# An audio tower on one core: two VectorE blocks merged, signs multiplied before they are searched for zeros, and the order inside a slot rewritten

## The chip, the cores and the metric

The kernel runs on one core of one Trainium2 chip. The metric is the device time of one execution in microseconds (us). PE is TensorE, DVE is VectorE, ACT is ScalarE.

## What is computed

Sixteen audio clips of 250 frames become a residual stream `h` (16 x 250 x 192). It passes top-k attention (A), a mixture of eight experts (B), a linear attention (C) and a mixture of sixteen experts (D). The change touches A and B.

```python
# A, per batch: 12 heads of 16, 250 queries by 250 keys
attn = jnp.einsum('bhnd,bhmd->bhnm', q, k) * SCALE
kth = jax.lax.top_k(attn, 100)[0][..., -1:]
attn = jax.nn.softmax(jnp.where(attn >= kth, attn, -jnp.inf), axis=-1)
h = h + einsum('bhnm,bhmd->bhnd', attn, v) @ w_proj + b_proj
# B: routed, on layernorm(h), the best 2 of 8 experts
gu = jnp.minimum(x @ Wgu + bgu, 7.0)
act = (jnp.maximum(up, -7.0) + 1.0) * gate * sigmoid(1.702 * gate)
h = h + sum over the chosen experts of score * (act @ Wd + bd)
```

## The kernel before

After the front end (to about 97 us) A and B run together in one program that every engine walks in the same order: `slots()`. A **unit** is four heads of one batch, so there are 48 units, and a **period** of four slots (s = 0 to 3) brings each unit one stage further. With k the age of a unit in periods:

- k = 0: PE computes scores, ACT copies them to `s_sb`.
- k = 1, slot 1: VectorE's `a_start` takes each row's maximum (`L1174`, 8 x 250 scores per partition) and from it and the mean a first threshold `first`; its last instruction (`L1187`) raises `start_set`, on which ACT waits.
- k = 1 to 4: ACT's `a_count` (`L919`) forms sign(threshold - score) for all scores and sums it; VectorE's `a_steps` (slot 0) moves the thresholds by interpolation. The fourth time the signs are kept, in bf16, in `mk` (8 x 250 per partition).
- k = 4, slot 1: VectorE's `a_rank`. `L1245` reads all 2000 signs, marks those equal to zero (a score that is exactly the threshold) and sums the marks in `ties`; `rank` says how far the count is from 100; seven small instructions turn both into `bad`, which is 0 where the threshold can be used. PE sums `bad` over the partitions (`L547`), VectorE copies the sum to `badi` (`a_flag`, slot 3).
- k = 5: `a_full` (slot 0) loads `badi` in a register and branches around an exact search that is needed if it isn't 0; then `a_hot` (`L1309`), and in every slot `a_top`: the 16 largest below the threshold by MAX, MATCH_REPLACE and MAX (`L1324`, `L1327`, `L1330`) for two of the eight rows. In even slots it begins with `L1320`, which prepares four rows. In odd slots it ends with `L1334` and `L1335`, which pick the 100th value (`kth`). `a_keep` (`L1344`) masks the exponentials with it; PE transposes the result (`L557`), ACT copies it, PE multiplies by v (`L571`).

In the same slots runs B, one of twelve steps per slot: PE multiplies up (`L457` with `w_b_g`, `w_b_u`), VectorE clips (`m0_first`: `L1425`, `L1428`), ACT takes the tanh, VectorE combines (`m0_act` `L1446`, `m0_weigh` `L1437`, `m0_hidden` `L1455`), PE multiplies down (`m0_down`, `L634`). `m0_act` and `m0_hidden` work on the step before that of `m0_first`. Twice per batch `residual` adds a result to `h` in five steps: add into `hb` (`L1139`), copy to `h` (`L1141`), two bn_stats, two bn_aggr, copy to `mv` (`L1117`).

The order on VectorE within a slot is that of the code. `Chain` guards instructions that use each other's results: `mark` lets an instruction raise a semaphore, `wait(but=k)` waits for all marked ones except the last k, `link` is both, `start` clears the semaphore (the row `ISA` in the listings below). `carry` is a one-element memset on which a wait rides.

Of the kernel before, what the change touches and what calls it, by code (L numbers as in the profile page):

```python
# [15 lines left out]
ALU = mybir.AluOpType  # L16
# [39 lines left out]
SHIFT = (WINDOW - 0.5) / 2  # L56
SLOPE = 1.0 / (2.7 * 193.2)
# [9 lines left out]
class Chain:  # L67
# [11 lines left out]
    def mark(self, ins):  # L79
        self.k += 1  # L80
        ins.then_inc(self.sem, 1)

# [79 lines left out]
def build(nc, d, out):  # L162
    with ExitStack() as ctx:
# [51 lines left out]
        st6 = sb("st6", [P, 2, 6])  # L215
        mvb = sb("mvb", [P, 2, 2])
# [35 lines left out]
        bad = own([P, 1], late)  # L252
        junk = own([P, UT * N // 2], late).bitcast(mybir.dt.bfloat16).rearrange("p (t n) -> p t n", t=UT)
# [839 lines left out]
        def _(dv):  # L1093
# [50 lines left out]

            dv.wait_ge(w_tok_ps, 1)
# [22 lines left out]
            def a_start(u):  # L1168

                n, ub = u[3:]  # L1170
                dv.wait_ge(s_set, UH * (n + 1))
                carry()
                top.start()
                top.link(dv.tensor_reduce(rowmax[:, ub, :], s_sb[:, ub, :, 0:N], AX.X, ALU.max))  # L1174
                way, mx = tiny[:, 0, :], rowmax[:, ub, :]
                top.mark(dv.tensor_scalar(nmx[:, ub, :], mx, -scale, None, ALU.mult))
                q = 1 - n_par(u)
                first, end = thr[:, q, 0, :], ends[:, q, :, 0, :]
                top.mark(dv.memset(end[:, Y_LO, :], FAR))
                top.mark(dv.memset(end[:, Y_HI, :], -FAR))  # L1180

                top.link(dv.scalar_tensor_tensor(way, s_sb[:, ub, :, N], -1.0 / N, mx, ALU.mult, ALU.add))
                top.link(dv.scalar_tensor_tensor(first, way, GUESS - 1.0, mx, ALU.mult, ALU.add))
                top.mark(dv.scalar_tensor_tensor(end[:, T_LO, :], way, -FAR * SLOPE, first,
                                                 ALU.mult, ALU.add))
                top.wait()
                dv.scalar_tensor_tensor(end[:, T_HI, :], way, FAR * SLOPE, first,  # L1187
                                        ALU.mult, ALU.add).then_inc(start_set, 1)

            def a_steps(b, g, p):  # L1190
# [15 lines left out]
                carry()  # L1206
                top.start()
# [25 lines left out]
            def a_rank(u):  # L1233


                n, ub = u[3:]
                m = n_par(u)
                dv.wait_ge(signs_set[3], n + 1)

                started = n + 4  # L1240
# [451 lines left out]
```

## Time and profile before

| | |
|---|---|
| runs of the kernel | 2815.48, 2818.47, 2827.93 us (median 2818.47) |
| the profiled execution | 2823.92 us, its span 2821.8 us |
| mean granted TensorE clock of the span | 0.825 |
| busy over the span | PE 2506.4 us (89%), DVE 1948.4 us (69%), ACT 1531.7 us (54%) |

The span has three parts: the front end, A with B (to about 1850 us), then C and D. The share of an engine over the whole says little; it has to be read by part. An instruction on VectorE can start before the one ahead of it has ended, so what one costs in a row of independent instructions is the distance between starts, not its duration.

### The profile page before, as it was taken

The page shows a single profiled execution, that of the slowest core. Times are in us where ns is not written, and L with a number is a line of the kernel's source. Part 1 is how long each engine was busy: PE and PEld are TensorE (multiplying, and loading weights), DVE is VectorE, ACT ScalarE, POOL GpSimd, SP SyncE. Part 2 cuts the span into 40 slices and gives each one's busy share as a digit, 9 for nine tenths or more (in the row PEclk, how much of TensorE's full clock was granted, in tenths as well). Part 3 has the DMA queues.
Part 4 walks back from the last instruction along what each step waited for, and adds up shares of the span by engine and source line. Part 5 has one row for each costly group of instructions (what it writes and reads, how often), then busy time and mean ns, then how long its engine had stood idle before and what let it go on. Part 6 is the DMA issues. An engine that isn't in the chain of part 4 may idle for free.

```text
span 2821.8 us, 39986 instructions
## 1 busy us (share of the span) xinstructions
PE 2506.4 (89%) x11650; PEld 2110.6 (75%) x11650; DVE 1948.4 (69%) x6490; ACT 1531.7 (54%) x4856; POOL 72.5 (3%) x45
## 2 busy tenths in 40 slices
PE   7778799898898898988888877899999899999999
PEld 3456677677776777777777767778887799999998
DVE  3278899999999999999999999864444232222222
ACT  1498887777777777777776774211111222222222
POOL 0000000000000000000000000000000110011110
PEclk9755567867778778778768777899999899999999
DMA  3000000000000000000000010130000000000000
GB/s 118 0 1 1 1 19 16 12 19 16 12 20 16 12 19 16 12 19 16 12 19 16 12 19 17 27 107 1 0 0 0 1 7 6 6 3 6 6 6 9
DMA packets 35000, 44.10 MB, mean 16 GB/s; under 512 B 6054, under 2 KB 33676, under 8 KB 34060
## 3 DMA queue, kind: packets, MB, share of 16 engines
q1 hardware_dynamic: 32208, 38.57, 5.4%
q10 hardware_dynamic: 2592, 3.33, 0.4%
q8 instruction: 69, 1.13, 0.2%
q14 instruction: 131, 1.07, 0.1%
HBM read 38.43 MB, written 3.20 MB: 15 GB/s over the span
## 4 chain that ended last, share of the span: by engine, by line
PE 41%; DVE 41%; issue 9%; ACT 6%; POOL 1%; DVEq 1%; DMA 0%; SPq 0%; ACTq 0%; POOLq 0%
PE bank L457 18%; PE bank L706 7%; DVE late L1327 4%; DVE late L1324 4%; DVE late L1344 3%; ACT late L919 3%; DVE late L1330 3%; DVE late L1245 3%; DVE late L1174 3%; DVE late L1320 3%; PE bank L536 2%; DVE extra L1455 2%; DVE extra L1446 2%; PE bank L767 2%; PE bank L571 2%
## 5 line engine op out<-in xcount | busy, mean ns | idle before, releaser
L919 ACT ACTIVATE late<-arena,late 125x250 bf16<-125x250 f32 x1152 | 561.3, 492 | 0.0
L1517 DVE TENSOR_TENSOR pair<-pair,arena 128x500 f32<-128x500 f32 x192 | 139.3, 726 | 443.1 <-PE bank L706 349.3
L571 PEld LDWEIGHTS bank<-vaug,late 125*125 125x125 f32 x1536 | 252.5, 240 | 167.1 <-ACT late L929 113.0
L457 PE MATMUL bank<-xT,late 128*128 128x250 f32 x1536 | 360.9, 378 | 0.0
L571 PE MATMUL bank<-vaug,late 125*125 125x17 f32 x1536 | 240.8, 293 | 120.8 <-ACT late L929 78.6
L536 PE MATMUL bank<-late 16*125 16x251 f32 x768 | 303.0, 530 | 21.3 <-ACT arena L896 20.4
L1033 ACT ACTIVATE pair<-bank 128x500 f32<-128x500 f32 x192 | 112.7, 587 | 382.5 <-PE bank L457 382.3
L457 PEld LDWEIGHTS bank<-xT,late 128*128 128x128 f32 x1536 | 287.0, 192 | 26.3
L706 PE MATMUL bank<-late,pair 128*125 128x192 f32 x1536 | 280.5, 326 | 0.0
L457 PE MATMUL bank<-extra,w_b_g 128*128 128x250 f32 x768 | 276.1, 495 | 0.8
L706 PEld LDWEIGHTS bank<-late,pair 128*125 128x125 f32 x1536 | 258.3, 187 | 9.5 <-DVE pair L1517 0.4
L457 PE MATMUL bank<-extra,w_b_u 128*128 128x250 f32 x768 | 255.2, 467 | 0.0
L937 ACT ACTIVATE late<-arena,late 125x250 f32<-125x250 f32 x384 | 171.2, 495 | 143.4 <-DVE late L1344 143.3
L557 PE MATMUL bank<-w_ident,late 125*125 125x125 f32 x768 | 164.6, 352 | 82.8 <-DVE late L1344 82.8
L536 PEld LDWEIGHTS bank<-late 16*125 16x125 f32 x768 | 172.4, 248 | 78.8 <-issue 31.4
L457 PEld LDWEIGHTS bank<-extra,w_b_g 128*128 128x128 f32 x768 | 176.4, 248 | 63.8 <-issue 33.9
L557 PEld LDWEIGHTS bank<-w_ident,late 125*125 125x125 f32 x768 | 147.9, 255 | 98.4 <-DVE late L1344 98.1
L919 ACT ACTIVATION_READ_ACCUMULATOR late<-arena,late 125x1 f32 x1152 | 220.1, 191 | 0.0
L457 PEld LDWEIGHTS bank<-extra,w_b_u 128*128 128x128 f32 x768 | 191.1, 249 | 34.9
L634 PE MATMUL bank<-w_b_d,extra 128*125 128x192 f32 x768 | 206.9, 402 | 0.6 <-DVE extra L1455 0.6
L919 ACT ACTIVATE pair<-arena,late 125x250 bf16<-125x250 f32 x384 | 187.7, 493 | 6.0 <-DVE late L1231 6.0
L1344 DVE SCALAR_TENSOR_TENSOR late<-arena,late 125x250 f32<-125x250 f32 x384 | 165.8, 474 | 3.8 <-DVE late L1335 0.5
(178 smaller groups left out, 3954.4 us busy)
## 6 DMA issues: line engine op xcount, KB each, us to landing
late<-comb_rows SPq DMA_DIRECT2D x128, 125.0 KB, 3.0
late<-comb_rows SPq DMA_DIRECT2D x128, 62.5 KB, 2.6
late<-in_d SPq DMA_DIRECT2D x1, 3072.0 KB, 9.9
out_h<-extra ACTq DMA_DIRECT2D x16, 187.5 KB
late<-in_d SPq DMA_DIRECT2D x1, 2304.0 KB, 14.9
arena<-in_frames SPq DMA_DIRECT2D x1, 1562.5 KB
w_b_g<-in_b_g SPq DMA_DIRECT2D x1, 1536.0 KB
w_b_u<-in_b_u SPq DMA_DIRECT2D x1, 1536.0 KB
```

What stands on the lines that cost most here:

```text
L457: ins = pe.matmul(dst, lhs(t), rhs(t), start=t == 0, stop=t == 1)
L536: ins = pe.matmul(bank[2][0:P, half * (N + 1):(half + 1) * (N + 1)], qk[r:r + DH, qk_slot(u), 0, half * P:half * P + P], qk[r:r + DH, qk_s ...
L557: ins = pe.transpose(bank[3][0:P, kh * N + half * P:kh * N + half * P + P], p_sb[:, s % 2, half, kh * P:kh * P + P], ident[0:P, 0:P])
L571: ins = pe.matmul(bank[4][0:P, at:at + VW], pT[:, s % 2, kh, half * P:half * P + P], vaug[:, p, kh, UH * g + s, :], start=kh == 0, stop=kh ...
L634: ins = pe.matmul(D[0:P, half * C:(half + 1) * C], hid0[:, s % 2, half * P:half * P + P], w["b_d"][:, s, :], start=False, stop=s == 11, sk ...
L706: ins = pe.matmul(D[0:P, half * C:(half + 1) * C], hid[:, s % 2, i, half * P:half * P + P], w["d_2"][:, 2 * s + i, :], start=(s == 0 and i ...
L919: ins = sc.activation(mk[:, n_par(u), t, :] if k == 3 else junk[:, t, :], s_sb[:, ub, t, 0:N], ACT.Sign, bias=thr[:, (n_par(u) + k + 1) % ...
L937: ins = sc.activation(e_sb[:, s % 2, half, :], s_sb[:, ub, t, 0:N], ACT.Exp, bias=nmx[:, ub, t:t + 1], scale=float(DH) ** -0.5)
L1324: top.mark(dv.max(m16[:, t, 0:8], work[:, t, :]))
L1327: top.mark(dv.match_replace(work[:, t, :], m16[:, t, 0:8], work[:, t, :], -BIG))
L1344: ins = dv.scalar_tensor_tensor(p_sb[:, s % 2, half, :], s_sb[:, ub, t, 0:N], kth[:, t:t + 1], e_sb[:, s % 2, half, :], ALU.is_ge, ALU.mult)
L1517: dv.tensor_tensor(hid[:, s % 2, :, :], gl[:, s % 2, :, :], c, ALU.mult).then_inc(hid_set[1], 1)
```

## The change

`a_start` and `a_rank` become one function, `a_start_and_rank`, whose instructions alternate; the search for zeros goes over products of four signs; the product is formed in two steps, 1000 and 500 wide. `a_load_flag` loads the register at the start of slot 0, ahead of `a_keep(last, 3)` and `a_steps`. `a_top` no longer waits at its end; `a_picked` and `a_thresholds` are its last two instructions, and `m0_act` comes between them. `m0_act`, `m0_weigh` and `m0_hidden` move from ahead of `a_top` to behind it. `add_to_h` takes the place of `residual` in A and B: it adds in place and writes `mv` without a copy. C keeps `residual`. Arithmetic on the other engines and their programs are the same.

```diff
+EDGE = (WINDOW / 2) ** 2 - ((WINDOW - 1) / 2) ** 2
...
+    def settle(self):
+        if self.k:
+            self.wait()
...
+            def add_to_h(ph, b, acc, ready, value, hs):
+                dv.wait_ge(ready, value)
+                hv = h[:, 2 * b:2 * b + 2, :].rearrange("p g c -> p (g c)")
+                dv.tensor_tensor(hv, hv, acc[0:P, 0:2 * C], ALU.add).then_inc(hs, 1)
+                stats.start()
+                dv.wait_ge(hs, b + 1)
+                ge(dv, stat_set[ph], b)
+                for half in (0, 1):
+                    stats.mark(dv.bn_stats(sums[ph - 1][:, half, :], h[:, 2 * b + half, :]))
+                stats.wait()
+                for half in (0, 1):
+                    ins = dv.bn_aggr(mv[ph][:, 2 * b + half, :], sums[ph - 1][:, half, :])
+                ins.then_inc(stat_set[ph], 1)
...
-            def a_start(u):
...
-            def a_rank(u):
...
+            def a_start_and_rank(u, r):
...
+                top.settle()
                 top.start()
+                if u:
...
+                    dv.wait_ge(s_set, UH * (n + 1))
+                    top.mark(dv.tensor_reduce(mx, s_sb[:, ub, :, 0:N], AX.X, ALU.max))
+                if r:
...
+                    dv.wait_ge(signs_set[3], nr + 1)
...
+                    four, two = UT * N // 2, UT * N // 4
+                    top.mark(dv.tensor_tensor(tied[:, 0:four], mks[:, 0:four], mks[:, four:2 * four], ALU.mult))
+                    top.mark(dv.tensor_scalar(rank[:, m, :], signs[:, 3, :], 0.5, TOPK - 1.0 - N / 2,
+                                              ALU.mult, ALU.add))
+                    top.wait(but=1)
+                    top.mark(dv.tensor_tensor(tied[:, four:four + two], tied[:, 0:two], tied[:, two:four], ALU.mult))
...
+                    top.wait(but=3 if u else 0)
+                    top.mark(dv.tensor_scalar(tied[:, four + two:2 * four], tied[:, four:four + two], 0.0, None,
+                                              ALU.is_equal, ALU.add, accum_out=ties[:]))
+                    top.mark(dv.scalar_tensor_tensor(places, rank[:, m, :], WINDOW - 1.0, rank[:, m, :],
+                                                     ALU.subtract, ALU.mult))
+                    top.wait(but=1)
+                    top.mark(dv.tensor_scalar(limit, ties[:], -SHIFT, EDGE, ALU.mult, ALU.add))
...
+                    top.mark(dv.tensor_scalar(spots[:], places, limit, None, ALU.is_ge, ALU.add, accum_out=outside))
...
+                    dv.scalar_tensor_tensor(bad[:], outside, FULL, ties[:],
+                                            ALU.mult, ALU.add).then_inc(bad_set, 1)
+                if u:
+                    top.wait()
+                    dv.scalar_tensor_tensor(end[:, T_HI, :], way, FAR * SLOPE, first,
+                                            ALU.mult, ALU.add).then_inc(start_set, 1)
...
+            def a_load_flag(u):
+                dv.wait_ge(bad_read, u[3] + 1)
+                dv.reg_load(flag, badi[0:1, 0:1])
...
                 if s == 0:
+                    if old:
+                        a_load_flag(old)
                     if last:
                         a_keep(last, 3)
...
                 if new:
                     m0_first(*new)
+                if old:
+                    a_top(old, s)
+                    if s % 2:
+                        a_picked(old, s)
                 if was:
                     m0_act(*was)
+                if old and s % 2:
+                    a_thresholds(old, s)
                 if new:
                     m0_weigh(*new)
                 if was:
                     m0_hidden(*was)
...
+                if old and s % 2:
+                    a_keep(old, s - 1)
+                if s == 1:
+                    a_start_and_rank(unit(i, g, p, 1), unit(i, g, p, 4))
```

VectorE, slot 1 of a period, from the masking (`L1344`) on; `late` holds the thresholds and small tiles, `pair` the signs, `arena` the scores. Before:

```order
L1344 SCALAR_TENSOR_TENSOR late<-arena,late 125x250
L1107 MEMSET carrier 1x1 [waits s_set]
L76 ISA
L1174 TENSOR_REDUCE late<-arena 125x8
L1176 TENSOR_SCALAR late<-late 125x8 [waits top_step]
...
L1187 SCALAR_TENSOR_TENSOR late<-late 125x8 [waits top_step]
L1107 MEMSET carrier 1x1 [waits start_set,signs_set3]
L76 ISA
L1245 TENSOR_SCALAR late<-pair 125x2000
L1247 TENSOR_SCALAR late<-late 125x8
L1251 TENSOR_SCALAR late<-late 125x8 [waits top_step]
```

After, at the same place:

```order
L1385 SCALAR_TENSOR_TENSOR late<-arena,late 125x250
L77 ISA [waits top_step]
L1247 TENSOR_REDUCE late<-arena 125x8 [waits s_set]
L1256 TENSOR_TENSOR late<-pair 125x1000 [waits signs_set3]
L1257 TENSOR_SCALAR late<-late 125x8
L1260 TENSOR_TENSOR late<-late 125x500 [waits top_step]
L1262 MEMSET late 125x8
L1263 MEMSET late 125x8
L1265 SCALAR_TENSOR_TENSOR late<-arena,late 125x8 [waits top_step]
L1268 TENSOR_SCALAR late<-late 125x500 [waits top_step]
L1270 SCALAR_TENSOR_TENSOR late<-late 125x8
L1273 TENSOR_SCALAR late<-late 125x1 [waits top_step]
```

The row of 2000 became rows of 1000, 500 and 500, with small instructions of both blocks between them. The rest of the block is six more small instructions; `bad` is the last but one of them, and the one that raises `start_set` is the last.

VectorE, an odd slot, from `m0_first` to the masking. Before:

```order
L1425 TENSOR_SCALAR late<-bank,w_b_bg 128x250 [waits gc_set,tanh_set,up_ps0,top_step]
L1428 TENSOR_SCALAR late<-bank,bup 128x250 [waits hid_set0]
L1446 SCALAR_TENSOR_TENSOR extra<-late 128x250 [waits hid_set0,gc_set,tanh_set]
L1437 TENSOR_TENSOR late<-late 128x250 [waits act_set,ring_set1,gate_set]
L1455 SCALAR_TENSOR_TENSOR extra<-late,extra 128x250 [waits down_ps0,u_set,act_set]
L76 ISA
L1324 MAX late<-late 125x8 x2
L1327 MATCH_REPLACE late<-late 125x250 [waits top_step] x2
L1330 MAX late<-late 125x8 [waits top_step] x2
L1334 TENSOR_TENSOR late<-hot,late 125x64 [waits top_step]
L1335 TENSOR_REDUCE late<-late 125x4 [waits top_step]
L1344 SCALAR_TENSOR_TENSOR late<-arena,late 125x250 [waits pt_ps,e_set,top_step]
```

After:

```order
L1466 TENSOR_SCALAR late<-bank,w_b_bg 128x250 [waits tanh_set,gc_set,up_ps0]
L1469 TENSOR_SCALAR late<-bank,bup 128x250 [waits hid_set0]
L77 ISA [waits top_step]
L1359 MAX late<-late 125x8 x2
L1362 MATCH_REPLACE late<-late 125x250 [waits top_step] x2
L1365 MAX late<-late 125x8 [waits top_step] x2
L1370 TENSOR_TENSOR late<-hot,late 125x64 [waits top_step]
L1487 SCALAR_TENSOR_TENSOR extra<-late 128x250 [waits hid_set0,gc_set,tanh_set]
L1375 TENSOR_REDUCE late<-late 125x4 [waits top_step]
L1478 TENSOR_TENSOR late<-late 128x250 [waits act_set,ring_set1,gate_set]
L1496 SCALAR_TENSOR_TENSOR extra<-late,extra 128x250 [waits down_ps0,u_set,act_set]
L1385 SCALAR_TENSOR_TENSOR late<-arena,late 125x250 [waits pt_ps,e_set,top_step]
```

The three instructions of B that follow `m0_first` (`L1446`, `L1437`, `L1455`; now `L1487`, `L1478`, `L1496`) moved behind the maxima, one of them into the gap of the chain that ends in the masking.

## Rows read from the trace of the kernel before

**Rows 1.** Busy time by stage; PEclk is the granted TensorE clock

```profile
core 0: us, PE busy (x) PEld busy (x) DVE busy (x) ACT busy (x) POOL busy (x), PEclk, DMA share, GB/s
170.00:280.00 110.00, 91.09 (x304) 70.69 (x304) 99.29 (x347) 95.64 (x343) 0.00 (x0) 0.53 0.00 1
800.00:1120.00 320.00, 280.40 (x1235) 230.49 (x1234) 301.06 (x1050) 242.86 (x831) 0.00 (x0) 0.78 0.07 16
1770.00:2820.00 1050.00, 997.51 (x5528) 904.54 (x5528) 397.17 (x1058) 254.30 (x510) 70.24 (x32) 0.97 0.04 12
```

**Rows 2.** Waits between 480 and 1656 us: us in total, times, longest

```profile
PE bank L557 <- DVE late L1344: 53.2, 29, 4.4
...
PE bank L571 <- DVE o_sb L1358: 38.7, 11, 4.8
```

**Rows 3.** The same view as rows 1 around one wait of TensorE

```profile
1016.00:1028.00 12.00, 12.00 (x69) 10.49 (x70) 11.36 (x33) 9.60 (x33) 0.00 (x0) 1.00 0.01 2
1035.00:1045.00 10.00, 7.22 (x20) 5.63 (x21) 8.88 (x38) 5.50 (x20) 0.00 (x0) 0.50 0.06 14
```

**Rows 4.** VectorE in order of time: start us, us; start and rank of one period

```profile
1015.69 2.23 DVE L1174 TENSOR_REDUCE late<-arena 125x8 f32<-125x2000 f32 x1
...
1019.07 2.24 DVE L1245 TENSOR_SCALAR_CACHE_REDUCE late<-pair 125x2000 bf16<-125x2000 bf16 x1
...
1021.23 0.17 DVE L1247 TENSOR_SCALAR late<-late 125x8 f32<-125x8 f32 x1
1021.44 0.17 DVE L1251 TENSOR_SCALAR late<-late 125x8 f32<-125x8 f32 x1
...
1022.51 0.87 DVE L1344 SCALAR_TENSOR_TENSOR late<-arena,late 125x250 f32<-125x250 f32 x2
```

**Rows 5.** The same view: small instructions without and with a wait between them

```profile
1039.26 0.17 DVE L1215 TENSOR_SCALAR side<-late 125x24 int32<-125x24 f32 x1
...
1039.34 0.17 DVE L1216 TENSOR_SCALAR side<-late 125x24 int32<-125x24 f32 x1
```

**Rows 6.** The same view: one residual with its statistics

```profile
1023.30 0.55 DVE L1139 TENSOR_TENSOR hb<-h,bank 125x384 f32<-125x384 f32 x1
1023.88 0.36 DVE L1141 COPY h<-hb 125x384 f32<-125x384 f32 x1
...
1025.20 0.48 DVE L1425 TENSOR_SCALAR late<-bank,w_b_bg 128x250 f32<-128x250 f32 x1
```

**Rows 7.** The same view: ends of an odd and of an even slot

```profile
1035.57 0.73 DVE L1330 MAX8 late<-late 125x8 f32<-125x250 f32 x2
1036.34 0.23 DVE L1334 TENSOR_TENSOR late<-hot,late 125x64 f32<-125x64 f32 x1
...
1036.85 0.87 DVE L1344 SCALAR_TENSOR_TENSOR late<-arena,late 125x250 f32<-125x250 f32 x2
...
1046.71 0.73 DVE L1330 MAX8 late<-late 125x8 f32<-125x250 f32 x2
1047.48 0.48 DVE L1425 TENSOR_SCALAR late<-bank,w_b_bg 128x250 f32<-128x250 f32 x1
```

**Rows 8.** The same view: before the branch of a_full

```profile
1040.94 0.18 DVE L1231 TENSOR_TENSOR late<-late 125x24 f32<-125x24 f32 x1
...
1041.96 0.29 DVE L1309 TENSOR_TENSOR hot<-w_iota,late 125x128 f32<-125x128 f32 x1 [0.84 <-issue]
```

**Rows 9.** VectorE groups until 1800 us, by form: busy us, mean ns, idle before

```profile
L1320 DVE SCALAR_TENSOR_TENSOR late<-pair,arena 125x1000 f32<-125x1000 bf16 x96 | 114.6, 1194 | 1.2 <-DVE hot L1309 0.2
L1245 DVE TENSOR_SCALAR_CACHE_REDUCE late<-pair 125x2000 bf16<-125x2000 bf16 x48 | 107.4, 2237 | 3.4 <-issue 0.4
```

**Rows 10.** VectorE, then TensorE, in order of time: one step of B and one wait

```profile
1026.63 0.41 DVE L1455 SCALAR_TENSOR_TENSOR extra<-late,extra 128x250 f32<-128x250 f32 x1
...
1032.62 0.89 PE L634 MATMUL bank<-w_b_d,extra 128*125 128x192 f32 x4
1037.78 1.20 PE L557 MATMUL bank<-w_ident,late 125*125 125x125 f32 x4 [4.26 <-DVE late L1344]
```

More of the change, by code:

```diff
@@ L215, in build @@
         st6 = sb("st6", [P, 2, 6])
+        sums = [sb(f"sums{i}", [P, 2, 6]) for i in range(2)]
         mvb = sb("mvb", [P, 2, 2])
@@ L252, in build @@
         bad = own([P, 1], late)
+        spots = sb("spots", [P, UT])
         junk = own([P, UT * N // 2], late).bitcast(mybir.dt.bfloat16).rearrange("p (t n) -> p t n", t=UT)
@@ L1166, in _ @@
             scale = float(DH) ** -0.5
-            def a_start(u):
[L1170 to L1188, printed above, removed]
             def a_steps(b, g, p):
@@ L1274, in a_full @@
                 m = n_par(u)
-                dv.wait_ge(bad_read, n + 1)
-                carry()
-                dv.reg_load(flag, badi[0:1, 0:1])
                 with dv.If_ne(flag, 0):
@@ L1307, in a_hot @@
                 m = n_par(u)
+                top.settle()
                 top.start()
@@ L1317, in a_top @@
                 m = n_par(u)
+                top.settle()
                 top.start()
@@ L1330, in a_top, with a_picked, a_thresholds @@
                     top.mark(dv.max(m16[:, t, 8:16], work[:, t, :]))
+            def a_picked(u, s):
                 top.wait()
-                if s % 2:
-                    two = slice(2 * s - 2, 2 * s + 2)
-                    top.link(dv.tensor_tensor(picked, hot[:, two, :], m16, ALU.mult))
-                    top.link(dv.tensor_reduce(kth[:, two], picked, AX.X, ALU.add))
+                top.mark(dv.tensor_tensor(picked, hot[:, 2 * s - 2:2 * s + 2, :], m16, ALU.mult))
+            def a_thresholds(u, s):
+                top.wait()
+                top.mark(dv.tensor_reduce(kth[:, 2 * s - 2:2 * s + 2], picked, AX.X, ALU.add))
             def a_keep(u, s):
                 n, ub = u[3:]
+                top.wait()
                 dv.wait_ge(e_set, UH * n + s + 1)
@@ L1471, in _ @@
                 if b is not None:
-                    residual(2, b, bank[6], down_ps[0], 12 * b + 12, h_set["B"])
+                    add_to_h(2, b, bank[6], down_ps[0], 12 * b + 12, h_set["B"])
                 b = at_slot(T, LG_AT + 1)
@@ L1486, in _ @@
                     m0_hidden(*was)
-                if old:
-                    a_top(old, s)
-                    if s % 2:
-                        a_keep(old, s - 1)
-                if s == 1 and unit(i, g, p, 1):
-                    a_start(unit(i, g, p, 1))
-                if s == 1 and unit(i, g, p, 4):
-                    a_rank(unit(i, g, p, 4))
+                if old and s % 2:
+                    a_keep(old, s - 1)
+                if s == 1:
+                    a_start_and_rank(unit(i, g, p, 1), unit(i, g, p, 4))
                 if s == 3 and unit(i, g, p, 4):
@@ L1497, in _ @@
                 if g == 0 and s == 2 and has(i - 3):
-                    residual(1, i - 3, bank[0], proj_ps[0], i - 2, h_set["A"])
+                    add_to_h(1, i - 3, bank[0], proj_ps[0], i - 2, h_set["A"])
                 b = at_slot(T, X_AT - 1)
```

47 lines of the change are left out of this document (27 added, 20 removed).

## The prediction, made before the changed kernel ran

> **What bounds the kernel now.** First the busy time by stage [rows 1]. From 170 us to about 1770 us VectorE is busy 90 to 94% of the time, TensorE 83 to 88%, ScalarE 76 to 87%. What VectorE is short of 100% there is made of gaps of 0.03 to 0.1 us behind waits on its own instructions; no wait for another engine in the rows of its timeline. So VectorE sets the pace of A and B. After 1770 us TensorE is busy 95% at a granted clock of 0.97 and VectorE 38%: nothing that VectorE saves there comes back, and before 170 us VectorE waits for ScalarE's signs. The stage in which a saving counts is 1600 us long.
>
> Second, what TensorE has in reserve, because it is next. Between 480 and 1656 us it waits 53.2 us for the masking and 38.7 us for `divide`, the latter 11 times, once per batch [rows 2]. A batch is three units, so that is 92 us in about 33 units, **2.8 us per unit**. Third, the clock. TensorE runs at full speed while it is busy (1.00 from 1016 to 1028 us), and after a wait of 4.26 us [rows 10] the next ten microseconds are granted 0.50, the lower of its two levels, 1.2 GHz [rows 3]. Its waits are therefore dearer than they look, and fewer waits would make it faster.
>
> **The change part by part**, in time of VectorE, per unit or slot. The unit of account is the distance between starts. A small instruction behind a wait on the one before it starts 0.20 us after it (1021.23 to 1021.44 in [rows 4]); without one 0.08 us (1039.26 to 1039.34 in [rows 5]).
>
> *Start and rank.* Before: from `L1174` at 1015.69 to the masking at 1022.51, 6.82 us [rows 4]. The search over 2000 signs takes 2.24 us of it, the maximum 2.23; the rest is a chain of linked small instructions. After: the maximum, 2.15 (next start); then the product of 1000 signs. The trace has no bf16 x bf16 product. Upper bound: `L1320`, 1000 elements in 1.19 us [rows 9]; with 2.24 for 2000 this is 1.04 per 1000 and 0.15 fixed. Lower bound: twice that rate, 0.67 us, as the copy of 384 (0.36) against the sum of 384 out of a bank (0.55) shows that VectorE can stream at double rate [rows 6]. I take the lower, since both inputs and the output are 2 bytes wide and the doubling is seen here even for 4-byte data. Product: 0.67 and 0.03 for the wait; the second, 500 wide, 0.26 + 0.15 = 0.41; then two memsets and `way` in its shadow, 0.13 beyond its next start; the search over 500 at single rate (it carries a sum, and `L1245` with its sum ran at single rate), 0.67, with the read of the sum 0.08; then `limit`, `first`, `nmx`, `spots` with its sum, `T_LO`, `bad`, `T_HI`, of which each has a neighbour to cover its wait: about 0.8. Sum 2.15 + 0.70 + 0.33 + 0.21 + 0.70 + 0.8 = 4.9 us, 1.9 less than 6.82. With the single rate for both products it is 0.78 more, 1.1 saved. Of 48 periods with a start, 44 have also a rank and lie behind 170 us: **84 us**. Three ranks without a start save about 1.1 each, since the chain of seven behind the search becomes four: **3 us**.
>
> The Trainium skill's page "VectorE: DVE Perf Modes", in its section on the perf-mode tier table, gives tensor_tensor on bf16 in SBUF double rate (1224 ns against 2293 ns for 2048 elements). No row here shows it for a product; by it the 4.9 stands, by the nearest row, `L1320`, it would be 5.7.
>
> *Sums into h.* Before, start to start, 1.90 us [rows 6]. After: 0.55 + 0.03, two statistics and their wait 0.65, two aggregates 0.18 = 1.4. Saved 0.48: the copy to `h` (0.36) and that to `mv`. About 28 of 32 lie in the stage: **13 us**. `h_set` also comes 0.4 us earlier for TensorE.
>
> *Odd slots.* Before, from the last pair of maxima at 1035.57 to the masking at 1036.85 are 1.28 us, of which the maxima hold 0.77 [rows 7]; the two linked instructions cost 0.51. After, the first starts 0.03 after the maxima end and the next instruction can follow after 0.15; the second, with `m0_act` between, 0.14. Saved 0.22, in the 82 odd slots in which B runs too: **18 us**. *Even slots.* The wait at the end of `a_top` (0.77 from 1046.71 to 1047.48) goes, since `m0_act` needs nothing of it: the start can be at 0.65. Saved 0.12 x 82: **10 us**.
>
> *The register.* Between `L1231` and `L1309` lie 1.0 us, 0.84 of it idle [rows 8], with the load of `badi` and a branch over the exact search. The branch stays. The load now stands right behind `a_flag`, whose result it waits for, and behind it on VectorE's queue stand the masking `a_keep(last, 3)` and all of `a_steps`; TensorE waits for that masking. So the load is moved from one bare spot to another, except in the third of the units in which `b_normalise` stands between. I take a third of the idle time, 0.3 us, in 16 units: **5 us**; bounds 0 and 0.35 x 48 = 17. The removed memsets (`carry`) overlap others and are counted at nothing.
>
> Sum: 84 + 3 + 13 + 18 + 10 + 5 = **133 us**, if all of VectorE's saving becomes time.
>
> *What takes some back.* Per unit of the steady stretch this is 1.9 + 0.3 + 0.44 + 0.24 + 0.1 = 3.0 us, a little over TensorE's 2.8. At an unchanged clock TensorE would bind, and 0.2 us x 33 units (7 us) be lost; and its waits are not evenly spread: only 29 masked heads of 132 in the stretch had one [rows 2]. In the others VectorE will sometimes find TensorE late. Against that stands the clock, which should fall less often. I take off 10%, 15 us in all. **Gain 118 us.** Of 2823.92 us (the profiled execution, span 2821.8) this leaves 2706; the median of the runs is 5.5 us lower, so the forecast for the median is **2700 us**, 4.2% faster.
>
> **The rivals.**
>
> *TensorE takes over.* For it: 88% busy, 2.8 us of reserve. If only half of the waits can be turned into time, because the clock stays at 0.78, the gain per unit is 1.4 to 1.8 us over 42 units, 60 to 75 us: 2750 us. Against it: all its waits end in VectorE's work, which comes earlier, and the clock recovers once it is busy [rows 3].
>
> *The products run at single rate.* 0.78 x 44 = 34 us less: 2734 us.
>
> *Order is worth nothing.* Then only removed work counts: per period 2.24 us of search become 0.67 + 0.41 + 0.67, three small instructions fewer (0.5), together about 1.0 x 44, and the copies, 13: 57 us, 2761 us. Against it stand 0.20 and 0.08 us in [rows 4, 5]. "VectorE: DVE Perf Modes" says this under "The DRAIN you can't avoid": chained operations pay the same with and without semaphores, so one should save operations, not waits. By that section the time would be this rival's; the rows disagree for instructions as small as these.
>
> *Slower: B's result comes late.* `m0_hidden` now stands behind `a_top`, in even slots 4.3 us later (1.2 for `L1320`, 3.1 for the rest). `m0_down` waits for it: in the shown slot it began 5.6 us after the result (1026.63 + 0.41 to 1032.62, [rows 10]), so 1.3 us would be left. If TensorE comes to both even slots too early, it waits there and its clock falls to 0.50; ten low microseconds as in [rows 3] cost it 5 us of work, so twice per unit 10 us, against 2.8 of reserve and 3.0 saved: such a unit gets 4.2 us longer. In every second unit of 42 that is 21 x 4.2 = 88 us more, less 59 us, the half of the gain: 2848 us. It decides from the point where the wait is longer than the one it has for the masking right after; against it, in odd slots the masking itself stands behind `m0_hidden`, so nothing is later than it was.
>
> That the change doesn't find what the old search found is no case: `rank * (rank - 15) >= 7.75 - 7.75 * ties` is the old test with 56.25 taken off both sides, and a product of four signs is zero if one is.
>
> **How the numbers follow.** Forecast 0.66; TensorE takes over 0.16; single rate 0.08; order worth nothing 0.05; slower 0.05. Own range of the forecast: full 133 us with the register's 12 more, 2673, to 2730. Reaching the second, third and fourth case the range is 2670 to 2762; the slower case and the outer tails are left out. A measurement can tell about 0.5% (14 us). Faster by more than that: 0.92; within 0.04; slower 0.04.
>
> **What would show it.** In the changed profile: the product of 1000 at 0.67 us (or 1.19); 4.9 us from the maximum's start to the masking; 1.4 us per sum into `h`; 0.15 us from the pick to `m0_act`; VectorE still over 90% busy to about 1650 us, TensorE above 92%, its clock there at 0.78 or higher. Wrong, if VectorE shows waits for `L457` of B's gate and up products or for the sum in bank 6, if TensorE waits at `L634` for `m0_hidden`, if the clock in the stretch is lower, or if ScalarE's counting waits for `start_set`, which is now raised last in its block, 1.8 us later against the maximum.

## The result, and the profile after

The changed kernel takes **2683.86 us** (median; 2682.34 to 2691.15) against 2823.2 us for the kernel before in the same comparison (2815.48 to 2829.24). The ratio is 0.9513, interval 0.948 to 0.9546: 4.9% faster, 139 us. The forecast was 2700 us, a gain of 118 us, with a range of 2670 to 2762. The profiled execution of the changed kernel took 2691.15 us, the slowest of its four, with a span of 2689.1 us.

The page of the changed kernel, its first rows and the granted clock in 40 slices:

```profile
span 2689.1 us, 39761 instructions
...
PE 2431.5 (90%) x11650; PEld 2052.7 (76%) x11650; DVE 1836.2 (68%) x6330; ACT 1527.3 (57%) x4856; POOL 72.7 (3%) x45
...
PEclk9975578888788878868877778999997999999999
```

Busy time by stage, the view of [rows 1]; A with B now ends 134 us earlier (last product of B at 1747 us instead of 1881), so the last stretch is taken from 1650:

```profile
core 0: us, PE busy (x) PEld busy (x) DVE busy (x) ACT busy (x) POOL busy (x), PEclk, DMA share, GB/s
170.00:280.00 110.00, 90.95 (x302) 70.80 (x302) 93.11 (x340) 97.04 (x343) 0.00 (x0) 0.53 0.00 1
800.00:1120.00 320.00, 297.67 (x1355) 247.14 (x1356) 305.26 (x1123) 264.07 (x908) 0.00 (x0) 0.80 0.07 16
1650.00:2690.00 1040.00, 986.24 (x5487) 894.65 (x5486) 384.13 (x1017) 250.15 (x500) 70.36 (x32) 0.98 0.04 12
```

VectorE is busy 95% of the middle stretch (94% before), TensorE 93% (88%), ScalarE rises too, and the clock is 0.80 instead of 0.78. Over the longer stretch from 480 to 1500 us it was 0.76 before (view of [rows 1]):

```profile
480.00:1500.00 1020.00, 900.93 (x3920) 738.41 (x3919) 959.74 (x3333) 769.81 (x2622) 0.00 (x0) 0.76 0.07 16
```

and is 0.80 now, with TensorE busy 942.50 us of it. The first stage shows no gain for anybody: there VectorE's busy share fell from 90 to 85% and the stage did not get shorter. More on that below.

The waits between 480 and 1536 us, the view of [rows 2] (us in total, times, longest):

```profile
PE bank L579 <- ACT late L937: 50.3, 38, 3.6
...
PE bank L565 <- DVE late L1385: 28.6, 20, 3.6
...
DVE hot L1343 <- DVE late L1232: 8.5, 25, 0.5
...
DVE late L1385 <- DVE badi L1298: 5.4, 11, 0.5
...
DVE late L1466 <- PE bank L465: 2.3, 1, 2.3
...
PE bank L579 <- DVE o_sb L1399: 0.8, 1, 0.8
```

and two lines of the kernel before that [rows 2] leaves out:

```profile
PE bank L571 <- ACT late L929: 31.2, 24, 3.2
...
DVE extra L1455 <- PE bank L634: 2.9, 4, 1.1
```

TensorE's wait for the masking went from 53.2 to 28.6 us, that for `divide` from 38.7 us in 11 waits to 0.8 us in one. Its wait for ScalarE's copy of the transposed result went the other way, from 31.2 to 50.3 us. VectorE's waits for TensorE rose from 2.9 us to about 6 in all, the longest 2.3 us, and there are two small gaps around the register load.

The merged block in order of time (start us, us), where [rows 4] had 6.82 us:

```profile
1021.60 2.23 DVE L1247 TENSOR_REDUCE late<-arena 125x8 f32<-125x2000 f32 x1
1023.75 0.67 DVE L1256 TENSOR_TENSOR late<-pair 125x1000 bf16<-125x1000 bf16 x1
...
1024.45 0.42 DVE L1260 TENSOR_TENSOR late<-late 125x500 bf16<-125x500 bf16 x1
...
1024.90 0.68 DVE L1268 TENSOR_SCALAR_CACHE_REDUCE late<-late 125x500 bf16<-125x500 bf16 x1
...
1025.50 0.16 DVE L1270 SCALAR_TENSOR_TENSOR late<-late 125x8 f32<-125x8 f32 x1
1025.62 0.15 DVE L1273 TENSOR_SCALAR late<-late 125x1 f32<-125x1 f32 x1
...
1026.17 0.17 DVE L1291 SCALAR_TENSOR_TENSOR late<-late 125x8 f32<-125x8 f32 x1
1026.29 0.87 DVE L1385 SCALAR_TENSOR_TENSOR late<-arena,late 125x250 f32<-125x250 f32 x2
```

4.69 us from the maximum to the masking. The product of 1000 takes 0.67 us, the double rate, and the one of 500 0.42. The search of 500 runs at single rate, 0.68. The small instructions behind it start 0.07 to 0.14 us apart.

A sum into `h`, against [rows 6]:

```profile
1057.54 0.55 DVE L1157 TENSOR_TENSOR h<-h,bank 125x384 f32<-125x384 f32 x1
1058.12 0.62 DVE L1162 BATCH_NORM_STATS2 sums<-h 125x6 f32<-125x192 f32 x2
1058.78 0.25 DVE L1165 BATCH_NORM_AGGREGATE mv<-sums 125x2 f32<-125x6 f32 x2
1058.94 0.44 DVE L1466 TENSOR_SCALAR late<-bank,w_b_bg 128x250 f32<-128x250 f32 x1
```

1.40 us instead of 1.90. And the end of an odd slot, against [rows 7]:

```profile
1035.12 0.72 DVE L1365 MAX8 late<-late 125x8 f32<-125x250 f32 x2
1035.88 0.23 DVE L1370 TENSOR_TENSOR late<-hot,late 125x64 f32<-125x64 f32 x1
1036.02 0.41 DVE L1487 SCALAR_TENSOR_TENSOR extra<-late 128x250 f32<-128x250 f32 x1
1036.35 0.21 DVE L1375 TENSOR_REDUCE late<-late 125x4 f32<-125x64 f32 x1
1036.48 0.41 DVE L1478 TENSOR_TENSOR late<-late 128x250 f32<-128x250 f32 x1
```

From the last maxima to the pick 0.76 us, then `m0_act` 0.14 later and, behind the sum over the pick, `m0_weigh` 0.13 later. The pick and its sum now take 0.27 us where they took 0.51.

### The profile page after: what moved, and what is told of

Its sections match the earlier page's. It is cut to its first block, busy times and chain, and to the rows that moved or that the text cites. A ratio compares the mean times of both kernels' runs of the same rounds, so it can differ in the third digit from the quotient of the medians.

```text
span 2689.1 us, 39761 instructions
## 1 busy us (share of the span) xinstructions
PE 2431.5 (90%) x11650; PEld 2052.7 (76%) x11650; DVE 1836.2 (68%) x6330; ACT 1527.3 (57%) x4856; POOL 72.7 (3%) x45
## 4 chain that ended last, share of the span: by engine, by line
PE 44%; DVE 34%; ACT 9%; issue 8%; POOL 2%; DVEq 1%; DMA 1%; another core or an unknown queue 0%; SPq 0%; ACTq 0%; POOLq 0%
PE bank L465 20%; PE bank L714 7%; ACT late L927 5%; DVE late L1362 4%; DVE late L1359 3%; DVE late L1385 3%; PE bank L544 3%; DVE late L1355 3%; DVE late L1247 2%; DVE late L1469 2%; DVE late L1365 2%; DVE extra L1496 2%; PE bank L579 2%; POOL arena L447 2%; PE bank L775 2%
## 5 line engine op out<-in xcount | busy, mean ns | idle before, releaser
L927 ACT ACTIVATE late<-arena,late 125x250 bf16<-125x250 f32 x1152 | 561.5, 494 | 0.0
L579 PEld LDWEIGHTS bank<-vaug,late 125*125 125x125 f32 x1536 | 241.3, 231 | 153.5 <-ACT late L937 139.3
L579 PE MATMUL bank<-vaug,late 125*125 125x17 f32 x1536 | 233.7, 288 | 106.3 <-ACT late L937 105.4
L544 PE MATMUL bank<-late 16*125 16x251 f32 x768 | 295.8, 519 | 20.6 <-ACT arena L904 19.7
L465 PE MATMUL bank<-extra,w_b_g 128*128 128x250 f32 x768 | 261.9, 474 | 2.4 <-DVE late L1469 2.4
L465 PE MATMUL bank<-extra,w_b_u 128*128 128x250 f32 x768 | 241.3, 446 | 0.0
L927 ACT ACTIVATION_READ_ACCUMULATOR late<-arena,late 125x1 f32 x1152 | 221.5, 192 | 0.0
L465 PEld LDWEIGHTS bank<-extra,w_b_g 128*128 128x128 f32 x768 | 168.2, 237 | 60.9 <-issue 34.6
L465 PEld LDWEIGHTS bank<-extra,w_b_u 128*128 128x128 f32 x768 | 181.4, 236 | 31.3
L565 PE MATMUL bank<-w_ident,late 125*125 125x125 f32 x768 | 153.8, 335 | 52.6 <-DVE late L1385 52.5
L927 ACT ACTIVATE pair<-arena,late 125x250 bf16<-125x250 f32 x384 | 187.6, 492 | 15.9 <-DVE late L1233 15.7
L642 PE MATMUL bank<-w_b_d,extra 128*125 128x192 f32 x768 | 192.4, 379 | 0.8 <-DVE extra L1496 0.8
L565 PEld LDWEIGHTS bank<-w_ident,late 125*125 125x125 f32 x768 | 139.2, 240 | 62.8 <-DVE late L1385 62.4
```

The costliest lines, as they stand in the source:

```text
L465: ins = pe.matmul(dst, lhs(t), rhs(t), start=t == 0, stop=t == 1)
L544: ins = pe.matmul(bank[2][0:P, half * (N + 1):(half + 1) * (N + 1)], qk[r:r + DH, qk_slot(u), 0, half * P:half * P + P], qk[r:r + DH, qk_s ...
L565: ins = pe.transpose(bank[3][0:P, kh * N + half * P:kh * N + half * P + P], p_sb[:, s % 2, half, kh * P:kh * P + P], ident[0:P, 0:P])
L579: ins = pe.matmul(bank[4][0:P, at:at + VW], pT[:, s % 2, kh, half * P:half * P + P], vaug[:, p, kh, UH * g + s, :], start=kh == 0, stop=kh ...
L642: ins = pe.matmul(D[0:P, half * C:(half + 1) * C], hid0[:, s % 2, half * P:half * P + P], w["b_d"][:, s, :], start=False, stop=s == 11, sk ...
L927: ins = sc.activation(mk[:, n_par(u), t, :] if k == 3 else junk[:, t, :], s_sb[:, ub, t, 0:N], ACT.Sign, bias=thr[:, (n_par(u) + k + 1) % ...
```

## The experiments

Differences are in medians. r0_after, e1, e2 and e3 ran together, e4, e5, e6 and e8 together, e9 to e12 together, each group with its own runs of the kernel before. Only the first group had the changed kernel in it. The differences of the other two are taken against the same 2682 to 2684 us and are uncertain by some 5 us more; by the ratios to the kernel before they come out a little otherwise, and where that matters it is said. As a second measure the text gives the time from the start of the 11th unit's maximum to that of the 48th, 37 units, in each profile: 1308.8 us in the kernel before, 1188.2 and 1185.8 us in the two profiles of the changed one, thus **3.3 us per unit** gained.

### The base again

> The changed kernel once more, beside the others of this group, as the base for their differences. Ratio to the kernel before 0.951 within 0.003.

Measured: 2682.25 us, ratio 0.9503 (0.9468 to 0.9538). The differences below are against this value.

### The products alone, taken out and put in

```diff
-  top.mark(dv.tensor_tensor(tied[:, 0:four], mks[:, 0:four], mks[:, four:2 * four], ALU.mult))
+  top.mark(dv.tensor_scalar(tied, mks, 0.0, None, ALU.is_equal, ALU.add, accum_out=ties[:]))
...
-  top.mark(dv.tensor_tensor(tied[:, four:four + two], tied[:, 0:two], tied[:, two:four], ALU.mult))
-  top.mark(dv.tensor_scalar(tied[:, four + two:2 * four], tied[:, four:four + two], 0.0, None,
-                            ALU.is_equal, ALU.add, accum_out=ties[:]))
```

> The changed kernel with the products taken out: one search over all 2000 signs, in the merged block. In the changed profile the two products and the search of 500 hold 1.75 us from start to start with three small instructions in their shadow; a whole search takes 2.16 and the three small ones 0.25, so 0.65 us more per unit. Theory (VectorE sets the pace): 0.65 x 47 = 31 us slower than the changed kernel. Rival (TensorE or ScalarE has taken over in many units): 0 to 15 us slower. Rival (the products are the main part of the 139 us): 70 us slower.

Measured: 2702.85 us, ratio 0.9569 (0.9534 to 0.9603), 21 us slower than the changed kernel; 1209.1 us for the 37 units, 0.6 us per unit. That is the expected size per unit. That it doesn't amount to 31 us is because it counts in 37 units and not 47.

The other way round, the products put into the kernel before, in its linked chain:

```diff
+  top.mark(dv.tensor_tensor(tied[:, 0:four], mks[:, 0:four], mks[:, four:2 * four], ALU.mult))
   top.mark(dv.tensor_scalar(rank[:, m, :], signs[:, 3, :], 0.5, TOPK - 1.0 - N / 2, ALU.mult, ALU.add))
+  top.wait(but=1)
+  top.link(dv.tensor_tensor(tied[:, four:four + two], tied[:, 0:two], tied[:, two:four], ALU.mult))
+  top.link(dv.tensor_scalar(tied[:, four + two:2 * four], tied[:, four:four + two], 0.0, None,
+                            ALU.is_equal, ALU.add, accum_out=ties[:]))
```

> The kernel before with the products alone, in its linked chain. Theory: 2.37 us from the search to the second instruction after it become 0.70 + 0.45 + 0.80 = 1.95; 0.42 x 47 = 20 us faster than before, ratio 0.993. Rival (products bring their full 1.4 us of streaming): 65 us faster, 0.977.

Measured: 2802.69 us, ratio 0.9933 (0.9914 to 0.9952), 16 us faster than the kernel before in its group; 1294.2 us for the 37 units, 0.4 us per unit. So the products, one of the three things in the change's title, are between an eighth and a seventh of its effect (16 us put in, 21 taken out, of 139). An estimate from the rows shows why: at 1.04 ns per element for the search and 0.50 for a product, streaming falls from 2.08 to 1.27 us, 0.8 less, but there are two more instructions, each with about 0.15 us of fixed time and a wait. They take back half of it.

### The order in the block

```diff
-  if s == 1:
-      a_start_and_rank(unit(i, g, p, 1), unit(i, g, p, 4))
+  if s == 1 and unit(i, g, p, 1):
+      a_start(unit(i, g, p, 1))
+  if s == 1 and unit(i, g, p, 4):
+      a_rank(unit(i, g, p, 4))          # both as before, the search with products
```

> The changed kernel with start and rank as two functions again, each instruction waiting for the one before, but with the products. Theory (waits between small instructions cost 0.12 us each and VectorE sets the pace): the pair takes 6.4 us instead of 4.7, 1.7 x 44 = 75 us slower than the changed kernel. Rival (order is worth nothing, only the removed instructions count): 10 us slower.

Measured: 2743.95 us, ratio 0.9711 (0.9675 to 0.9747), 62 us slower; 1246.1 us for the 37 units, 1.6 us per unit. Its timeline:

```profile
1013.26 2.23 DVE L1242 TENSOR_REDUCE late<-arena 125x8 f32<-125x2000 f32 x1
...
1016.23 0.17 DVE L1255 SCALAR_TENSOR_TENSOR late<-late 125x8 f32<-125x8 f32 x1
...
1016.63 0.68 DVE L1273 TENSOR_TENSOR late<-pair 125x1000 bf16<-125x1000 bf16 x1
...
1018.51 0.17 DVE L1282 TENSOR_SCALAR late<-late 125x8 f32<-125x8 f32 x1
1018.72 0.17 DVE L1283 TENSOR_TENSOR late<-late 125x8 f32<-125x8 f32 x1
...
1019.58 0.66 DVE L1136 TENSOR_SCALAR xn<-h,mv,rstd 125x192 f32<-125x192 f32 x2
```

6.32 us from the maximum to the next piece of work, against 4.69. The streaming is the same in both; the difference is 0.20 us steps (1018.51 to 1018.72) where the merged block has 0.07 to 0.14, a gap of 0.40 us between the two blocks (1016.23 to 1016.63), and two small instructions more (seven instead of five in the rank, since the old test is back with the old order), besides two one-element memsets. At 0.20 us each those two explain 0.4 of the 1.6 us per unit, some 15 of the 62 us (an estimate; it was not run apart). The rest, about 45 us, is the order. Merging is the largest part of the change, and the rival by which order is worth nothing, which had 10 us for this run, is out. For small dependent instructions the sentence of the Trainium skill's page "VectorE: DVE Perf Modes" in "The DRAIN you can't avoid", that the semaphore costs nothing extra, does not hold here: on 8 elements the next start is 0.20 us away behind a wait on the instruction just before, and 0.07 us where nothing has to be waited for.

### The order in the slot

```diff
   if new:
       m0_first(*new)
-  if old:
-      a_top(old, s)
-      if s % 2:
-          a_picked(old, s)
   if was:
       m0_act(*was)
-  if old and s % 2:
-      a_thresholds(old, s)
   if new:
       m0_weigh(*new)
   if was:
       m0_hidden(*was)
+  if old:
+      a_top(old, s)
+      if s % 2:
+          a_picked(old, s)
+          a_thresholds(old, s)
```

> The changed kernel with the instructions of B ahead of the maxima again and the pick and its sum linked; the wait at the end of the even slots stays away. Theory: 0.24 us in 82 odd slots, 20 us slower than the changed kernel. Rival (B's later result costs TensorE waits that this takes back): 0 to 10 us, or even faster. VectorE's waits for TensorE at the sum of step 12 and the clock would tell.

Measured: 2701.66 us, ratio 0.9569 (0.9535 to 0.9603), 19 us slower, 0.5 us per unit. This is the 0.24 us twice per unit, as expected. This run has the same instructions as the changed kernel, in another order, and so is the cleanest proof that order counts. The later result of B costs TensorE nothing that shows, and the rival built on it is out.

### The sums into h, and the register

e4 puts `residual` back in both places.

> The changed kernel with residual instead of add_to_h in A and B. Theory: 0.5 us x 28 = 14 us slower than the changed kernel (ratio to before about 0.956). Rival (hidden): within 5 us.

Measured: 2691.74 us, ratio 0.9541 (0.9524 to 0.9557), 9 us slower (11 by the ratios); 1194.5 us for the 37 units, 0.2 us per unit. That is between the expected 14 and the rival's 5.

```diff
   if s == 0:
-      if old:
-          a_load_flag(old)
       if last:
           a_keep(last, 3)
       a_steps(i, g, p)
       if old:
+          a_load_flag(old)
           a_full(old)
```

> The changed kernel with the register loaded right before the branch again. Theory (the load moved from one bare spot to another): 2 us slower than the changed kernel, -3 to +6. Rival (the early load is hidden): 0.33 x 47 = 15 us slower.

Measured: 2694.42 us (2684.11 to 2700.95), ratio 0.9559 (0.9533 to 0.9586), 12 us slower by the medians, but with a scatter of that size; 1195.7 us for the 37 units, 0.2 us per unit. What the load does in the changed kernel its timeline shows:

```profile
1037.92 0.14 DVE L1298 CAST badi<-bank 1x1 int32<-1x1 f32 x1
1038.55 0.87 DVE L1385 SCALAR_TENSOR_TENSOR late<-arena,late 125x250 f32<-125x250 f32 x2 [0.49 <-DVE badi L1298]
...
1041.03 0.18 DVE L1233 TENSOR_TENSOR late<-late 125x24 f32<-125x24 f32 x1
1041.70 0.29 DVE L1343 TENSOR_TENSOR hot<-w_iota,late 125x128 f32<-125x128 f32 x1 [0.49 <-DVE late L1232]
```

0.49 us idle ahead of the masking, and 0.67 us from `L1233` to `a_hot`, which were 1.0 us [rows 8]. The load was moved from one bare spot to another, with a small gain on balance. Between 480 and 1500 us VectorE stands idle 21.8 us ahead of `a_hot` in e6; in the changed kernel it is 11.1 us there and 8.2 ahead of the masking, so by the gaps the gain is some 3 us. By the medians it is 12, outside the expected -3 to +6 and close to the rival's 15. Which is right stays open; both lie within 0.5%.

### Covering the load and the branch

```diff
   if s == 0:
-      if old:
-          a_load_flag(old)
       if last:
           a_keep(last, 3)
+      if old:
+          a_load_flag(old)
       a_steps(i, g, p)
-      if old:
-          a_full(old)
-          a_hot(old)
...
   if new:
       m0_first(*new)
+  if old and s == 0:
+      a_full(old)
+      a_hot(old)
```

> The changed kernel with the load behind the masking of slot 0 (0.87 us of VectorE work cover it) and the branch and a_hot behind m0_first (0.86 us cover it). Theory (VectorE still sets the pace): 0.5 us before a_hot and 0.26 before the masking go, 30 to 36 us faster than the changed kernel, ratio to before about 0.94. Rival (TensorE's reserve is used up): 0 to 12 us faster, with waits of VectorE for TensorE's up products.

Measured: 2671.28 us (2659.89 to 2674.78), ratio 0.9457 (0.9429 to 0.9486), 11 us faster than the changed kernel. The expected 30 to 36 us were missed by a factor of three, and the measured value lies in the rival's range, 0 to 12 us. A batch is three units; the batches that run undisturbed, which are most of them, now take 93.1 instead of 94.5 us, 0.5 us per unit and not 0.7: behind `a_hot` there is a new gap. And VectorE waits for TensorE (VectorE's waits from 480 to 1600 us):

```profile
DVE late L1466 <- PE bank L465: 9.2, 4, 3.6
DVE late L1355 <- DVE hot L1343: 7.8, 35, 0.6
DVE lg L1416 <- PE bank L465: 3.5, 2, 2.0
DVE h L1157 <- PE bank L642: 3.2, 2, 1.6
```

16 us of them are for TensorE (`L1466`, `lg`, `h`), against 5 in the changed kernel. The edit's own saving is about 17 us in the 37 units; the waits take the larger part of it back.

### Has TensorE any reserve?

e9 gives TensorE more work and e10 less; in both, VectorE's program is that of the changed kernel.

```diff
+  for _ in range(4):
+      pe.matmul(bank[2][0:P, 504:512], ident[0:P, 0:P], ident[0:P, 0:8], start=True, stop=True)
```

> The changed kernel with four more TensorE transposes of 125 rows by 8 columns in every slot of a unit's scores (their result is not used), 16 per unit, at 0.19 to 0.33 us each 3 to 5 us more TensorE work per unit, over its idle time of 2.8 us per unit (9% of 31.6). Theory (TensorE has reserve, and its clock rises when it waits less): 0 to 25 us slower than the changed kernel. Rival (TensorE is at its end): its work beyond the idle time adds up, 45 to 100 us slower.

Measured: 2782.99 us (2751.33 to 2789.14), ratio 0.9815 (0.9751 to 0.988), some 100 us slower than the changed kernel (88 by the ratios). The theory's 0 to 25 us were missed and the rival's 45 to 100 met: TensorE's work beyond what it has idle adds up.

```diff
-  ins = two_k(bank[5 + 2 * (s % 2)][:, i * N:(i + 1) * N],
-              lambda t: w[name][:, t, 128 * s:128 * s + 128], lambda t: xTb[:, b % 2, t, :])
+  ins = pe.matmul(bank[5 + 2 * (s % 2)][:, i * N:(i + 1) * N],
+                  w[name][:, 0, 128 * s:128 * s + 128], xTb[:, b % 2, 0, :], start=True, stop=True)
```

> The changed kernel with half of the products of B's gate and up (the second part of the sum over inputs is left out), four of eight 250-column products per slot, 1 to 2 us less per slot on TensorE. VectorE's work is the same. Theory (VectorE sets the pace to 1650 us): only the few waits go that VectorE still has for TensorE, about 5 to 10 us, and the stretch after the last unit, 80 us at TensorE's pace, gets some 15 us shorter: 15 to 25 us faster than the changed kernel. Rival (both engines limit): 40 us or more.

Measured: 2666.23 us, ratio 0.944 (0.9416 to 0.9464), 17 us faster, as the theory had it: with this much less work for TensorE, VectorE still sets the pace. For the stretch from 480 to 1500 us, the busy times (columns as in [rows 1]) of the changed kernel:

```profile
480.00:1500.00 1020.00, 942.50 (x4299) 777.14 (x4298) 979.92 (x3571) 841.48 (x2878) 0.00 (x0) 0.80 0.08 17
```

of e9, and VectorE's wait in it:

```profile
480.00:1500.00 1020.00, 1003.14 (x5068) 875.29 (x5068) 928.85 (x3379) 800.46 (x2756) 0.00 (x0) 0.80 0.07 16
```

```profile
DVE late L1468 <- PE bank L465: 66.3, 29, 6.4
```

and of e10:

```profile
480.00:1500.00 1020.00, 943.24 (x3805) 780.03 (x3805) 982.95 (x3581) 844.65 (x2900) 0.00 (x0) 0.68 0.07 17
```

This is the row to remember. With 494 recorded products fewer, TensorE is busy for the **same** 943 us, because its clock is granted at 0.68 instead of 0.80; and the 37 units take 1183.1 us against 1188.2 and 1185.8. A busy share of 92% would have said that there are 8% of reserve in one as in the other. With more work (e9) TensorE is busy 98%, and the clock stays at 0.80: it doesn't rise further when the last waits go. The 37 units take 1264.4 us, 2.1 us more each, for TensorE work of 34.2 x 0.983 - 32.1 x 0.924 = 4.0 us more each. The difference, **1.9 us per unit, is the reserve** that TensorE has left in the changed kernel, for work added at this place. VectorE sets the pace there, but only just. Of the 100 us, 76 come in the 37 units and 21 already between the first and the eleventh, which says something of the first stage (see below).

e11 joins e8 and e10.

> The load and the branch covered, and the same half of TensorE's products of B left out. If TensorE is what kept that edit from its 30 us (16 us of VectorE's waits for it in the stretch), this is 25 to 32 us faster than the changed kernel with the half left out, where the edit alone brought 11. If the edit itself is worth no more, 10 to 15.

Measured: 2665.07 us, ratio 0.9425 (0.9397 to 0.9452), 1 us faster than e10 (5 us by the 37 units, 1177.9 against 1183.1). Both expected values, 25 to 32 and 10 to 15, were missed: taking work from TensorE did not set the edit's saving free. VectorE's waits show why this test tells less than I thought:

```profile
DVE h L1158 <- PE bank L643: 6.9, 3, 4.9
DVE late L1467 <- PE bank L626: 3.3, 2, 2.8
```

With less work the clock is lower, and at a lower clock TensorE is again late at single places, here at the sum of B and its first step. That accounts for 10 us; why the rest of e8's saving doesn't show stays open.

e12 is e8 with `a_hot` moved behind the maxima of slot 0.

> The load and the branch covered, and a_hot moved behind the maxima of slot 0 without a wait of its own. The profile of the version before it shows 0.21 us idle between a_hot and the preparation of four rows, and a_hot's 0.29 can overlap: 0.3 us x 46 = 14 us less VectorE work. Theory (VectorE sets the pace): 10 to 14 us faster than that version, ratio to before 0.941. Rival (TensorE takes over): within 5 us of it.

```diff
   if old and s == 0:
       a_full(old)
-      a_hot(old)
   if old:
       a_top(old, s)
+      if s == 0:
+          a_hot(old)          # top.mark instead of settle, start and link
```

Measured: 2666.86 us, ratio 0.9443 (0.9412 to 0.9475), 4 us faster than e8, where 10 to 14 were expected and the rival had "within 5". The runs of both spread over 12 to 15 us, so the 4 us are not clear of the noise. Undisturbed batches take 92.2 us, but VectorE waits 19 us for TensorE. By the medians this version is the fastest of those that compute everything, 0.6% below the changed kernel, whose interval in r0_after (0.9468 to 0.9538) it just touches.

## Why the prediction was right, and where it was off

**The bound.** Right for units 11 to 48, and wrong for the first ten. The forecast let VectorE bind from 170 us, because it was busy 90% and its rows showed no waits for others. The 11th unit starts at the same time in both kernels (its maximum, in order of time). Row of before:

```profile
347.69 2.23 DVE L1174 TENSOR_REDUCE late<-arena 125x8 f32<-125x2000 f32 x1
```

and of after:

```profile
348.24 2.23 DVE L1247 TENSOR_REDUCE late<-arena 125x8 f32<-125x2000 f32 x1
```

None of the 2.1 us of the block and 0.5 us of the slot came back up to there. The chain of waits from 170 to 345 us, by line, of before:

```profile
by line: ACT late L919 31.2%; ACT pair L919 8.5%; PE bank L571 7.8%; PE bank L536 7.2%; ACT late L937 6.8%; issue 6.5%; PE bank L457 5.2%; PE bank L557 3.6%; ACT arena L896 3.0%; ACT late L929 2.1%; PE bank L464 1.6%; DVE late L1284 1.3%; D
```

and of after:

```profile
by line: ACT late L927 31.3%; ACT pair L927 10.6%; ACT late L945 7.5%; issue 7.0%; PE bank L579 6.8%; PE bank L544 6.8%; PE bank L465 3.5%; ACT arena L904 3.4%; PE bank L565 3.1%; ACT late L937 1.9%; PE bank L472 1.6%; DVE late L1317 1.3%; 
```

ScalarE's sign passes (`L919`, now `L927`) lead in both, 31% and another 9 to 11% for those written to `pair`; TensorE's lines together have 25 and 22%, and no line of VectorE has more than 1.3%. ScalarE was busy 87% [rows 1], TensorE 83% at a granted clock of 0.53. In e9 the work added to TensorE makes this stage longer too: from the first unit's maximum to the eleventh's 270.4 us instead of 249.7. Its chain:

```profile
by line: ACT late L929 20.7%; PE bank L546 14.6%; PE bank L544 12.1%; PE bank L581 12.0%; ACT pair L929 8.6%; PE bank L567 6.2%; issue 5.0%; ACT late L947 3.6%; PE bank L465 2.1%; PE bank L472 1.6%; ACT late L939 1.4%; DVE late L1319 1.3%; 
```

So ScalarE and TensorE share the lead there, and VectorE's full timeline was a consequence. No run took work from ScalarE; its part rests on the chain alone. This step put seven units x 3 us = 21 us too many in the forecast.

**The block** (1.9 x 44 = 84 us). The mechanism and every duration were right: 0.67 and 0.42 for the products, 0.68 for the search. The size was 2.13 us instead of 1.9. The eight small instructions behind the search took 0.79 us, as worked out (0.8); shorter were the stretch from the second product to the search, 0.45 us (0.33 and 0.21 in the sum), and the search with its read, 0.60 (0.70). Of this, e2 shows 62 us for the merging with two instructions less, and e1 21 us for the products; together the 84 us, by a larger saving in fewer units.

**Odd slots** (18 us). e3 shows 19. **Sums into h** (13 us). 0.50 us each as worked out, e4 shows 9. **The wait at the end of even slots** (10 us). 0.65 us from maxima to `m0_act` is there in the timeline (1010.84 to 1011.49 us of the changed kernel); not tried alone. **The register** (5 us). Between 3 and 12.

**What is taken back** (15 us). This was the term that was too large. VectorE's waits for TensorE in the stretch are about 6 us, and TensorE was not at its end: 1.9 us per unit were left. Two things made the room. First, the reserve was larger than the forecast counted. Beside the 2.8 us per unit of [rows 2], TensorE waited 31.2 us for ScalarE's copies and 13.3 for `h`, 4.1 us per unit in all. The waits for VectorE in [rows 2] fell from 2.8 us per unit to 0.9 (29.4 us over 1056 us), those for ScalarE rose from 0.9 to 1.5, and e9's 1.9 us show that most of this idle time can be used as well. Second, the clock did rise, as the forecast had it, from 0.76 to 0.80 between 480 and 1500 us: for the same products TensorE was busy 31.2 us per unit before (35.4 x 0.883) and 29.7 after (32.1 x 0.924). So of the 3.3 us that a unit got shorter, TensorE gave about half from its idle time and half from its busy time. Without the second it would have been busy 97% of the new time. What the forecast had wrong about the clock is the picture behind it. Its "full speed while it is busy" was read from one stretch of 12 us; just behind it TensorE is busy without a gap and has 0.50 (kernel before, view of [rows 1]):

```profile
1028.30:1031.50 3.20, 3.20 (x8) 2.48 (x8) 3.03 (x11) 3.20 (x13) 0.00 (x0) 0.50 0.15 28
```

Nor do the ten low microseconds of [rows 3] follow the wait of 4.26 us; they begin 1.5 us into it (the lower level was granted from 1035.0 to 1045.3 us, the wait began at 1033.5). And e9, with next to no waits, still has 0.80.

So the number came out closer than its terms, partly by luck: errors went against each other. The measured gain is 37 x 3.3 = 121 us in the stretch, 13 to 20 us after the last unit's start (1165.4 us from there to the end before, 1152.7 and 1144.8 after) and nothing in front. Against the forecast's 118 us: seven units that gave nothing, -21; 0.3 us more per unit in the other 37, +12; the 15 us taken off, +15; and 6 to 13 us more at the end than the 7 or so in the sum. That makes 130 to 137 us, beside the measured 139 with its 9 us of uncertainty.

**The rivals.** TensorE takes over: not in this change, but in e8, e11 and e12 it begins. Single rate: out, by the 0.67 us. Order is worth nothing: out, by e2 and e3. B's result comes late: out, by e3 and by the absence of any long wait at `L642`. Its working had `m0_hidden` 4.3 us later in even slots; the rows have 3.4 (from `L1320` at 1044.05 us to the end of the slot at 1047.48), so more room was left than the text thought. The 57 us of the third rival counted three small instructions fewer; there are two. Of the signs of being wrong, small ones appeared: a wait of 2.3 us for B's gate product, and in r0_after one of 1.1 us for the sum in bank 6; none of ScalarE for `start_set`.

## What to carry to other kernels

Where an engine runs chains of instructions on a few elements, look at the distances between starts: merging two independent chains so that each covers the other's waits brought more than twice what a faster search over 2000 elements brought. Before counting a saving, ask of each stage which engine's chain leads, not which engine is busy; a full engine can be fed at another's pace. And to learn whether TensorE has reserve, give it more work for one run: its busy time follows its clock and doesn't tell by itself.

## What was not expected of the hardware

- TensorE's busy time in a stretch of 1020 us was 943 us with 4299 recorded products and 943 us with 3805; the granted clock was 0.80 and 0.68.
- Kept busy 98% of the time in that stretch, TensorE was granted 0.80, the same as at 92%, while in C and D at 95% it is 0.98, and before the change, at 88%, it was 0.76. Whether another kind of added work would have changed that was not tried.
- On bf16, a search that carries a sum costs 1.04 ns per element (2.24 us for 2000, 0.68 for 500), a product of two tensors 0.50 ns (0.67 us for 1000, 0.42 for 500).
- A register load right behind the instruction whose result it reads holds up VectorE's queue for 0.49 us.
